# Decoder layer on one core: self-attention scores as one multiplication of 96 stacked rows per head with 256 columns each, and each unit one slot later

## The chip, the cores and the metric

One Trainium2 chip, one of its cores. The metric is the device time of one execution in microseconds (us); smaller is better.

## The reference

One pre-norm decoder layer in float32: x is (2, 1024, 512), the context (2, 2048, 512). The self-attention has 16 heads of 32 elements; each token sees only keys at an even distance of at most 16. Queries and keys are divided by their length before the scores.

```python
x = x + attn(layernorm(x))             # qkv projection, 16 heads, windowed softmax, output projection
x = x + cross_attn(layernorm(x), ctx)  # one head of 512, 1024 x 2048 scores per batch, full softmax
x = x + ffn(layernorm(x))              # silu(x wg) * (x wu), then wd; hidden size 1536

# inside attn, per head (d = 32):
q = q / (norm(q) + 1e-6); k = k / (norm(k) + 1e-6)
scores = q @ k.T                       # scale 1
allowed = (abs(j - i) <= 16) & ((j - i) % 2 == 0)
out = softmax(where(allowed, scores, -inf)) @ v
```

## The kernel before

The tokens are laid out so that even and odd positions are apart: four sequences (`NS` = 4 rounds, `s`) of 512 tokens (`SEQ`), in which the window is a plain band of 8 to either side. Each round has 16 heads in 4 groups of 4 (`g`), and 4 tiles of 128 keys (`i`). A **unit** is one group and one tile, `n = 4 g + i`; there are 16 units in a round and 64 in all. The key tile of a unit meets a window of 136 or 144 queries (`window(i)`).

Every float32 operand of a multiplication is split into a rounded part (`_h`) and its rest (`_l`), and a product is the sum of three: high by high, high by low, low by high (`three`, lines 189 to 191).

The program is written out by hand, engine by engine; each engine executes its own list in order, and waits on counted semaphores. The loop over the units is the skeleton: for each of TensorE (PE), VectorE (DVE), ScalarE (ACT), GpSimd (POOL) there is a **slot** `n` of round `s`, and each slot also holds pieces of other work:

- slots 0 to 3: `project_qk(s, 1, t)`, the second half of the round's query and key projection; 4 to 7: `project_v`, `project_out(s-1, t)` (the output projection of the round before), transposes of the next round's input; 8 to 11: `project_qk` of the next round, transposes for the cross-attention query; 12 to 15: `project_v` of the next round and `project_query(s-1, m)`; in the last round the first score blocks of the cross-attention (`cross.pe_scores`) start there.
- `heads(s, g)` turns a group's queries and keys on PE into two PSUM banks (`kt`, `qt`). `heads_hi` (ACT) and `heads_lo` (DVE) copy them out as high and low parts: `kt_h`, `kt_l`, and for the queries `qbd_h`, `qbd_l`, each in two copies that a mask (`hmask`) zeroes for every other head. Groups 2 and 3 are turned in slots 6 and 7, group 0 of the next round in slot 14, group 1 in slot 15.
- `scores(s, n)`: six multiplications. Two heads share 64 rows; the zeroed halves of `qbd` keep them apart. The pair for rows 0 to 63 and the one for rows 64 to 127 stand side by side, for each of the three products. Then `exp` (ACT) into `probs`, `mask` (POOL, line 508, times `band`), and `weighted(s, n)` (PE, lines 1179 and 1183): eight multiplications of 32 columns of the array, the values and the row sums.
- In slot `n` PE makes `scores(n + 1)` first and `weighted(n)` last; ACT and POOL likewise handle unit `n + 1`. Units 8 and the next round's 0 are made at the end of slots 7 and 15 (`LATE`).
- When a group is done, `copy_out` (ACT) takes sums and values to SBUF, `inverse` (DVE, line 906, two halves) inverts the sums, `out_scale` (POOL, line 517) multiplies, `out_hi` (ACT) and `out_lo` (POOL, line 522) split the result for `project_out`, which waits for the `out_lo` of group 3 of its round. `out_bias` (POOL, line 527) adds a bias to the residual rows; `root1` (POOL, lines 483 and 485) belongs to the next round's norm.
- `spread1`, `spread2` (DVE) are norm statistics, `scale_units` (POOL) divides by the lengths. The DMAs of the SP queue load `x_in` (next round's input), `xs` (residual rows), `ct_raw` (context) and store `x1_scratch`, `qp_scratch`. `cross.load_ct(sp, n)` waits for `ct_l` of block `n - 2`.

## Time and profile before

| what | value |
|---|---|
| runs | 1194.45 and 1193.20 us, median 1193.83 |
| profiled execution | 1193.53 us, span of its instructions 1191.5 us |
| self-attention with its projections | about 48 to 380 us of the span |
| PE busy | 97% of the span |
| granted TensorE clock | 0.991 of full speed on the mean |

The profiled execution is 2.0 us longer than its span. Busy time of PE counts multiplications whose ends are modelled and overlap; the distance between two starts tells more of its pace than the duration of one.

### The profile page before, as it was taken

To read this page: it belongs to the slowest core of one execution; us is meant where nothing else is said; L and a number is where in the kernel's file an instruction comes from. 1 tells how busy PE (TensorE), PEld (TensorE's weight loads), DVE (VectorE), ACT (ScalarE), POOL (GpSimd) and SP (SyncE) were. 2 spreads that over 40 slices of the span, in tenths; PEclk is the share of its full clock that TensorE was granted. 3 is DMA by queue.
4 is the path that set the end of the run, shared out by engine and by line. 5 is a ranking of instruction groups with operands and counts; after the bars stand their busy time and mean duration, and the time that the engine had idled before them with its cause. 6 is when DMAs were issued, how large, how long until landed. Compare 5 with 4: busy or idle time off the path is not lost.

```text
span 1191.5 us, 17227 instructions
## 1 busy us (share of the span) xinstructions
PE 1151.1 (97%) x6432; PEld 935.4 (79%) x6432; DVE 872.4 (73%) x1352; ACT 548.3 (46%) x862; POOL 431.7 (36%) x383
## 2 busy tenths in 40 slices
PE   7999999999989999999999997999999998999998
PEld 6777778777767888888888885878778887888886
DVE  6666675684684657876687798875899878888775
ACT  5354454455364345554445444554444445444431
POOL 1255765665753300200020034022445842444431
PEclk9899999999989999999999998999999999999999
DMA  8001010200133434333334332223311111511101
GB/s 292 9 28 45 10 63 1 80 37 23 50 111 130 166 132 142 115 101 142 121 125 149 116 121 73 80 80 123 124 54 54 54 53 63 170 53 53 53 18 71
DMA packets 53570, 103.88 MB, mean 87 GB/s; under 512 B 4848, under 2 KB 17136, under 8 KB 52464
## 3 DMA queue, kind: packets, MB, share of 16 engines
q1 hardware_dynamic: 53488, 102.78, 25.8%
q8 instruction: 52, 0.85, 0.3%
q14 instruction: 30, 0.25, 0.1%
HBM read 85.99 MB, written 16.78 MB: 86 GB/s over the span
## 4 chain that ended last, share of the span: by engine, by line
PE 81%; DVE 9%; ACT 4%; issue 3%; POOL 3%; ACTq 0%; DVEq 0%; POOLq 0%
PE work L189 15%; PE work L190 14%; PE work L191 14%; PE score L189 4%; PE score L190 4%; PE score L191 4%; PE score L2523 4%; PE score L2524 4%; PE score L2525 4%; PE score L1165 2%; PE work L2523 2%; PE work L2525 2%; PE work L2524 2%; PE score L1179 1%; PE work L1092 1%
## 5 line engine op out<-in xcount | busy, mean ns | idle before, releaser
L508 POOL TENSOR_TENSOR probs<-probs,band 128x544 f32<-128x544 f32 (+1 forms) x64 | 92.4, 1444 | 87.3 <-ACT probs L639 87.0
L2196 POOL TENSOR_TENSOR hid<-fg,hid 128x512 fp32r<-128x512 f32 x48 | 84.4, 1778 | 106.5 <-ACT hid L2263 106.5
L189 PE MATMUL score<-pt_h,cn_h 128*128 128x512 f32 x256 | 101.8, 398 | 9.5 <-DVE pt_l L1672 5.9
L1512 POOL TENSOR_TENSOR xr<-xr,bv_row 128x512 f32<-128x512 f32 x16 | 27.3, 1731 | 228.1 <-DMA xr<-x_scratch 228.1
L190 PE MATMUL score<-pt_l,cn_h 128*128 128x512 f32 x256 | 100.6, 393 | 0.0
L191 PE MATMUL score<-pt_h,cn_l 128*128 128x512 f32 x256 | 100.5, 393 | 0.0
L189 PE MATMUL work<-x_q_h,ct_h 128*128 128x512 f32 x256 | 100.3, 392 | 0.0
L191 PE MATMUL work<-x_q_h,ct_l 128*128 128x512 f32 x256 | 99.7, 389 | 0.0
L190 PE MATMUL work<-x_q_l,ct_h 128*128 128x512 f32 x256 | 99.7, 389 | 0.0
L2402 DVE SCALAR_TENSOR_TENSOR fx<-work,fx 128x512 f32<-128x512 f32 x96 | 65.7, 685 | 40.2 <-PE work L191 40.2
L189 PE MATMUL work<-wqkv_h,xt_h 128*128 128x512 f32 (+1 forms) x256 | 94.0, 367 | 0.0
L2523 PE MATMUL score<-fxt,w_hl 128*128 128x512 f32 x236 | 92.3, 391 | 1.5 <-DVE fxt L2350 0.8
L2525 PE MATMUL score<-fxt,w_hl 128*128 128x512 f32 x236 | 91.9, 389 | 0.0
L2524 PE MATMUL score<-fxt,w_hl 128*128 128x512 f32 x236 | 91.8, 389 | 0.0
L2184 POOL TENSOR_TENSOR wsum<-w_stage 128x256 f32<-128x256 f32 x24 | 18.4, 765 | 194.0 <-ACT w_stage L2220 138.3
L190 PE MATMUL work<-wqkv_l,xt_h 128*128 128x512 f32 (+1 forms) x256 | 87.5, 342 | 0.0
L191 PE MATMUL work<-wqkv_h,xt_l 128*128 128x512 f32 (+1 forms) x256 | 87.4, 342 | 0.0
L1566 ACT ACTIVATE x_pr<-x_s 128x512 f32<-128x512 f32 x52 | 33.0, 634 | 94.4 <-DVE x_s L1668 94.4
L2263 ACT CAST hid<-fg 128x512 fp32r<-128x512 f32 x48 | 29.7, 621 | 87.5 <-DVE fg L2387 52.8
L189 PE MATMUL work<-wd_h,hid 128*128 128x512 f32 x176 | 68.7, 391 | 0.6 <-DVE fx L2402 0.6
L1672 DVE TENSOR_TENSOR pt_l<-x_pr,pt_h 128x512 fp32r<-128x512 f32 x64 | 51.3, 802 | 24.4 <-ACT pt_h L1570 23.6
L191 PE MATMUL work<-wd_h,hid 128*128 128x512 f32 x176 | 68.5, 389 | 0.0
(254 smaller groups left out, 3176.1 us busy)
## 6 DMA issues: line engine op xcount, KB each, us to landing
ct_raw<-in_ctx_t SPq DMA_DIRECT2D x32, 512.0 KB, 4.6
cn_raw<-in_ctx_n SPq DMA_DIRECT2D x32, 512.0 KB, 3.8
w_stage<-in_wg_t SPq DMA_DIRECT2D x12, 512.0 KB, 4.1
w_stage<-in_wu_t SPq DMA_DIRECT2D x12, 512.0 KB, 3.8
wd_raw<-in_wd_t SPq DMA_DIRECT2D x12, 512.0 KB, 3.7
x_in<-in_x SPq DMA_DIRECT2D x16, 256.0 KB, 2.8
xs<-in_x SPq DMA_DIRECT2D x4, 1024.0 KB, 5.2
x_scratch<-xs SPq DMA_DIRECT2D x4, 1024.0 KB, 4.7
```

The costliest lines, as they stand in the source:

```text
L189: pe.matmul(out, hi_s, hi_m, start=first, stop=False)
L190: pe.matmul(out, hi_s, lo_m, start=False, stop=False)
L191: return pe.matmul(out, lo_s, hi_m, start=False, stop=last)
L508: PL.tensor_tensor(probs[:, n % 2, :, 0:w], probs[:, n % 2, :, 0:w], band[:, c0:c0 + w].unsqueeze(1).to_broadcast([P, HPG, w]), ALU.mult). ...
L1566: A.activation(pr[:, j % 2, :], s_at(j), ACT.Exp).then_inc(e_done, 1)
L1672: V.tensor_tensor(pt_l[:, j % 2, :], pr[:, j % 2, :], pt_h[:, j % 2, :].bitcast(F32), ALU.subtract)\
L2196: PL.tensor_tensor(hid[:, q, 1, :], g[:, q, :], hid[:, q, 0, :].bitcast(F32), ALU.subtract).then_inc(hidl_done, 1)
L2263: A.copy(hid[:, q, 0, :], g[:, q, :]).then_inc(hidh_done, 1)
L2402: V.scalar_tensor_tensor(xs[:, t, :], work[:, 2 + n % 2, :], WSCALE, xs[:, t, :], ALU.mult, ALU.add)\
L2523: PE.matmul(bank(key), w_h, x_h, start=first, stop=False, skip_group_check=True)
L2524: PE.matmul(bank(key), w_h, x_l, start=False, stop=False, skip_group_check=True)
L2525: last = PE.matmul(bank(key), w_l, x_h, start=False, stop=k == 1, skip_group_check=True)
```

## The change

The scores of one head become one multiplication. A new SBUF tensor `stack` holds, for each of the four heads, three blocks of 32 rows: on the key side high, low, high, on the query side high, high, low. One multiplication over these 96 rows gives the sum of the three products. It always has 256 query columns, and the exponential reads the window out of them. The blocks are put there by DMAs from the SP queue: `stack_heads(s, g, b)` issues 12 for each half `b` of the 512 columns (24 per group, 384 in all), each of 32 rows by 2 by 256 floats (64 KB). They wait until the group's `heads_lo` is done and until the scores of the group before have read that half. The masked copies and `hmask` are gone: ACT and DVE each handle one query tile where there were two.

Each unit's scores, exponential and mask stand one slot later, at the start of slot `n`; `weighted(n - 1)` is the last thing in slot `n`. `copy_out`, `inverse`, `out_scale`, `out_hi` and `out_lo` stand one slot later too. `out_bias`, `root1`, `project_out` and all other pieces stay in their slots.

```diff
@@ SyncE @@
+            def stack_heads(s, g, b):
+                k = group(s, g)
+                if b == 0:
+                    wait_freed(sp, ("qt", s, g))
+                if k:
+                    sp.wait_ge(s_ready, ST * (k - 1) + 3 + b)
+                c = slice(b * SEQ // 2, (b + 1) * SEQ // 2)
+                parts_of, (k_h, k_l, q_h, q_l) = turned_heads(g)
+                for h in range(HPG):
+                    r = slice(DH * h, DH * h + DH)
+                    for i, (of_k, of_q) in enumerate(((k_h, q_h), (k_l, q_h), (k_h, q_l))):
+                        sp.dma_start(stack[DH * i:DH * i + DH, h, :, c].bitcast(F32),
+                                     parts_of[r, of_k:of_q + 1:of_q - of_k, c].bitcast(F32)).then_inc(stacked[b], 16)
...
+                stack_heads(s, 3, 0)
+                if s == NS - 1:
+                    cross.load_ct(sp, 2)
+                stack_heads(s, 3, 1)
...
+                if s + 1 < NS:
+                    for b in range(2):
+                        stack_heads(s + 1, 0, b)
@@ GpSimd @@
                 for n in range(UN):
-                    if n not in LATE:
-                        mask(s, n + 1)
-                    if n == 1 and s:
+                    mask(s, n)
+                    if n == 2 and s:
                         out_scale(group(s, -1))
-                    if n == 2 and s:
+                    if n == 3 and s:
                         out_lo(group(s, -1))
                     if n in (2, 3) and s:
                         out_bias(s - 1, 2 * n - 4)
@@ ScalarE @@
-                A.copy(kt_h[:, g % 2, :], bank(("kt", s, g))).then_inc(kq_hi, 1)
+                A.copy(parts_of[:, k_h, :], bank(("kt", s, g))).then_inc(kq_hi, 1)
                 wait_filled(act, ("qt", s, g))
-                for j in range(2):
-                    A.mul(qbd_h[:, g % 2, j, :], bank(("qt", s, g)), hmask[:, j:j + 1]).then_inc(kq_hi, 1)
+                A.copy(parts_of[:, q_h, :], bank(("qt", s, g))).then_inc(kq_hi, 1)
...
-                        if n == 2 and s:
+                        if n == 3 and s:
                             out_hi(group(s, -1))
@@ VectorE @@
-                    if n in (0, 1) and s:
-                        inverse(group(s, -1), n)
+                    if n in (1, 2) and s:
+                        inverse(group(s, -1), n - 1)
@@ TensorE, scores @@
-                if i == 0:
-                    wait_freed(pe, ("qt", s, g))
+                if i < 2:
+                    pe.wait_ge(stacked[i], MOVED * (group(s, g) + 1))
...
-                for kt, qt, first_mm, last_mm in ((kt_h, qbd_h, True, False), (kt_h, qbd_l, False, False),
-                                                  (kt_l, qbd_h, False, True)):
-                    for a in range(2):
-                        r = slice(64 * a, 64 * a + 64)
-                        last = PE.matmul(out[a], kt[r, g % 2, c], qt[r, g % 2, :, lo:lo + w],
-                                         start=first_mm, stop=last_mm)
+                for h in range(HPG):
+                    out = scb[:, h // 2, SEQ // 2 * (h % 2):SEQ // 2 * (h % 2) + SEQ // 2]
+                    at = min(lo, SEQ // 2)
+                    last = PE.matmul(out, stack[0:3 * DH, h, 0, P * i:P * i + P], stack[0:3 * DH, h, 1, at:at + SEQ // 2],
+                                     start=True, stop=True)
@@ TensorE, slots @@
-                    if n not in LATE:
-                        scores(s, n + 1)
+                    scores(s, n)
...
-                    weighted(s, n)
+                    if n:
+                        weighted(s, n - 1)
+                    elif s:
+                        weighted(s - 1, UN - 1)
             s = NS - 1
+            weighted(s, UN - 1)
```

The program's order on PE, at the change from one slot to the next. Before:

```order
L1179 MATMUL score<-probs,v 32x144 x4
L1183 MATMUL score<-probs,ones 32x144 x4
L1165 MATMUL score<-qbd_h,kt_h 128x2x136 x2
L1165 MATMUL score<-qbd_l,kt_h 128x2x136 x2
L1165 MATMUL score<-qbd_h,kt_l 128x2x136 x2
L189 MATMUL work<-wqkv_h,xt_h 128x512
```

and in the changed kernel:

```order
L1206 MATMUL score<-probs,v 32x144 x4
L1210 MATMUL score<-probs,ones 32x144 x4
L1192 MATMUL score<-stack 128x256 x4
L189 MATMUL work<-wqkv_h,xt_h 128x512
```

Six multiplications in three pairs have become four single ones; the place between `weighted` and the projection is the same.

The order on POOL in slots 1 to 3 of a round after the first (`o_sc` is `out_scale`, `ot_l` is `out_lo`, `xs` is `out_bias`, `rstd` and `nb` are `root1`, `probs` is `mask`). Before:

```order
L517 TENSOR_TENSOR o_sc<-o_sc,rsum 128x512
L508 TENSOR_TENSOR probs<-probs,band 128x4x136
L522 TENSOR_TENSOR ot_l<-o_sc,ot_h 128x512
L527 TENSOR_TENSOR xs<-xs,ob_row 128x512 x2
L483 TENSOR_TENSOR rstd_155<-ve_153,mhalf 128x1
L485 TENSOR_SCALAR nb_157<-mv_151,rstd_155 128x1
```

and in the changed kernel:

```order
L554 TENSOR_TENSOR o_sc<-o_sc,rsum 128x512
L564 TENSOR_TENSOR xs<-xs,ob_row 128x512 x2
L520 TENSOR_TENSOR rstd_154<-ve_152,mhalf 128x1
L522 TENSOR_SCALAR nb_156<-mv_150,rstd_154 128x1
L545 TENSOR_TENSOR probs<-probs,band 128x4x136
L559 TENSOR_TENSOR ot_l<-o_sc,ot_h 128x512
```

`out_lo` of the last group, which followed `out_scale` and one mask, now follows two `out_bias` and one `root1` as well.

The order on the SP queue from the last part of round 0 to the first of round 1. Before:

```order
L429 DMA xs<-in_x 128x4x512
L392 DMA x_in<-in_x 128x512 x4
L396 DMA x_scratch<-xs 128x4x512
```

and in the changed kernel:

```order
L456 DMA xs<-in_x 128x4x512
L421 DMA stack<-heads_even 32x2x256 x12
L398 DMA x_in<-in_x 128x512
L421 DMA stack<-heads_even 32x2x256 x12
L421 DMA stack<-heads_ot 32x2x256 x24
L421 DMA stack<-heads_even 32x2x256 x24
L421 DMA stack<-heads_x2t 32x2x256 x24
L398 DMA x_in<-in_x 128x512 x3
```

The queue, which held nine issues there, now holds 24 more for every group.

## Rows read from the trace of the kernel before

**Rows 1.** The page: busy time of each engine, and the chain that ended last.
```profile
PE 1151.1 (97%) x6432; PEld 935.4 (79%) x6432; DVE 872.4 (73%) x1352; ACT 548.3 (46%) x862; POOL 431.7 (36%) x383
...
PE 81%; DVE 9%; ACT 4%; issue 3%; POOL 3%; ACTq 0%; DVEq 0%; POOLq 0%
```

**Rows 2.** Timeline of PE, end of slot 2, start of slot 3, round 2 (start, duration).
```profile
223.58 0.43 PE L1183 MATMUL score<-probs,ones 128*32 128x144 f32 x8
223.94 0.40 PE L1165 MATMUL score<-qbd_h,kt_h 64*128 64x272 f32 x2
...
224.52 0.50 PE L189 MATMUL work<-wqkv_h,xt_h 128*128 128x512 f32 x1
224.86 0.39 PE L190 MATMUL work<-wqkv_l,xt_h 128*128 128x512 f32 x1
```

**Rows 3.** Timeline of PE, where 256-column multiplications follow `weighted` directly.
```profile
204.92 0.39 PE L189 MATMUL work<-wqkv_h,xt_h 128*128 128x256 f32 x1
205.15 0.28 PE L190 MATMUL work<-wqkv_l,xt_h 128*128 128x256 f32 x1
205.26 0.28 PE L191 MATMUL work<-wqkv_h,xt_l 128*128 128x256 f32 x1
```

**Rows 4.** Timeline of PE: starts that later steps are measured against.
```profile
93.83 0.40 PE L1165 MATMUL score<-qbd_h,kt_h 64*128 64x288 f32 x2
...
125.94 0.40 PE L1165 MATMUL score<-qbd_h,kt_h 64*128 64x288 f32 x2
...
230.18 0.40 PE L189 MATMUL work<-wo_h,ot_h 128*128 128x512 f32 x1
230.42 0.40 PE L190 MATMUL work<-wo_l,ot_h 128*128 128x512 f32 x1
...
359.56 0.40 PE L1165 MATMUL score<-qbd_h,kt_h 64*128 64x288 f32 x2
```

**Rows 5.** Timeline of DVE, slots 1 and 2 of round 2.
```profile
220.89 1.74 DVE L906 RECIPROCAL rsum<-rsum 128x256 f32<-128x256 f32 x1
...
223.42 0.69 DVE L852 TENSOR_TENSOR qk<-work,qkb_row 128x512 f32<-128x512 f32 x1 [0.25 <-PE work L191]
224.04 0.69 DVE L815 BATCH_NORM_STATS2 stats<-x_in 128x6 f32<-128x512 f32 x1
```

**Rows 6.** Timeline of POOL, slots 1 to 3 of round 2.
```profile
222.71 1.29 POOL L517 TENSOR_TENSOR o_sc<-o_sc,rsum 128x512 f32<-128x512 f32 x1 [4.18 <-DVE rsum L906]
223.95 1.37 POOL L508 TENSOR_TENSOR probs<-probs,band 128x544 f32<-128x544 f32 x1
...
226.62 2.53 POOL L527 TENSOR_TENSOR xs<-xs,ob_row 128x512 f32<-128x512 f32 x2
229.11 0.55 POOL L483 TENSOR_TENSOR rstd<-ve,mhalf 128x1 f32<-128x1 f32 x1
229.75 0.27 POOL L485 TENSOR_SCALAR nb<-mv,rstd 128x1 f32<-128x1 f32 x1
```

**Rows 7.** Timeline of the SP queue: start, time to issue, count.
```profile
0.79 1.33 SPq L403 DMA_DIRECT2D x_in<-in_x  x3
...
230.90 0.33 SPq L392 DMA_DIRECT2D x_in<-in_x  x1
...
355.69 0.33 SPq L1445 DMA_DIRECT2D ct_raw<-in_ctx_t  x1
```

**Rows 8.** The page, DMA issues: count, KB each, median us to landing.
```profile
x_scratch<-xr SPq DMA_DIRECT2D x16, 256.0 KB, 2.1
```

**Rows 9.** Timeline of DVE, `heads_lo` of round 0 group 2 and round 1 group 0.
```profile
87.36 0.69 DVE L895 TENSOR_TENSOR kt_l<-work,kt_h 128x512 fp32r<-128x512 f32 x1 [0.98 <-ACT kt_h L628]
...
119.84 0.69 DVE L895 TENSOR_TENSOR kt_l<-work,kt_h 128x512 fp32r<-128x512 f32 x1
```

**Rows 10.** Windows: stretch, length, busy times, then PEclk, DMA share, GB/s.
```profile
345.00:349.00 4.00, 1.26 (x22) 0.84 (x22) 2.07 (x6) 3.35 (x6) 3.02 (x3) 1.00 0.00 0
...
351.00:355.00 4.00, 4.00 (x10) 3.17 (x11) 3.93 (x5) 1.81 (x4) 1.92 (x2) 0.50 0.00 0
```

More of the change, by code:

```diff
@@ L364, in attention_phase @@
     kq_hi = sem("kq_hi")
+    stacked = [sem(f"stacked{b}") for b in range(2)]
     s_ready = sem("s_ready")
@@ L554, in _ @@
                         root2(s - 1, n - 6)
-                    if n in (6, 9, 13):
-                        out_scale(group(s, n // 4 - 1))
-                    if n == 7:
-                        mask(s, 8)
                     if n in (7, 10, 14):
-                        out_lo(group(s, {7: 0, 10: 1, 14: 2}[n]))
-                    if n == 15 and more:
-                        mask(s + 1, 0)
+                        out_scale(group(s, {7: 0, 10: 1, 14: 2}[n]))
+                    if n in (8, 11, 15):
+                        out_lo(group(s, {8: 0, 11: 1, 15: 2}[n]))
             s = NS - 1
```

104 lines of the change are left out of this document (53 added, 51 removed).

## The prediction

> **What bounds the kernel now.** I read the page first: PE is busy 97% of the span and carries 81% of the chain that ended last [rows 1]. So a change on DVE, ACT, POOL or the DMAs counts only where PE comes to wait for it, and a change on PE counts in full. I then read PE's timeline by starts, because the durations overlap, and looked for the distance between neighbours. Last I read DVE, POOL and the SP queue in the slots where the change reorders them, against the moment at which PE needs the result.
>
> **PE itself.** From the row sums of `weighted` to the second multiplication of the next piece the profile has 223.58 to 224.86 = 1.28 us: 0.36 to the scores, 0.58 for them, 0.34 to the second projection multiplication [rows 2]. The three pairs of 64 rows are cheap, but they change the shape of the tile in use twice, and each change costs at both sides: the multiplications of 256 columns that follow `weighted` directly start 0.36 us after the row sums as well, are then 0.23 us apart once and 0.11 to 0.12 us after that [rows 3]. For the new form I take 96 rows to be the same kind of tile as 128 rows. Then the new form is 0.36 to the first of the four, 0.23 + 0.12 + 0.12 + 0.12 to the projection's start, and 0.24, the undisturbed distance of 512 columns [rows 4], to its second multiplication: 1.19 us, 0.09 less than now. Times 64 units that is 5.8 us. The eight units that stood at the end of slots 7 and 15 lose one more change of tile, 0.1 us on each of its sides by the same rows, 1.6 us. Together **-7 us**, all on the path. If 96 rows count as a shape of their own, the change into projection work stays (0.34 in place of 0.24, and 0.1 more ahead of it): 0.2 us x 64 = 13 us dearer than that, **+6 us**. I take -7: the only tiles in the rows whose change costs are those of 64 rows and of 32 columns, and 96 rows fit into neither half.
>
> The Trainium skill bears on this on both sides. Its page TensorEngine Tiling (Array Packing), section Key Properties, says that changing the tiling mode drains the engine; the 0.34 us above against 0.24 agrees. The Trainium skill's page TensorE: Matmul & The Clock Gate, Part 3, advises to put small contractions on separate row groups, where they run at once, which speaks against this change: by columns alone the old form streams 3 x 280 and the new one 4 x 256, 184 more, so by that rule alone the sum would have +5 us in place of -7.
>
> DVE and ACT lose one tile of 128x512 per group, 0.7 us each (one such piece takes 0.69 [rows 9]); they are not the bound, so I count that at nothing except in the latency of `heads_lo` below.
>
> **`out_lo` of the last group, in rounds 1 to 3.** `project_out` of slot 4 waits for it, and starts now at 230.18 with no wait [rows 4]. Now the halves of `inverse` lie in slots 0 and 1; the second starts at 220.89 and `out_scale` follows at 222.71 [rows 5, 6]. After the change the second half is in slot 2. There DVE takes up the projection's tile at 223.42, the statistics from 224.04 for 0.69 + 0.4 us, then the inverse for 1.74: it ends at 226.85 [rows 5]. POOL then makes `out_scale` (1.29), two `out_bias` (2.53), `root1` (0.87 from 229.11 to 229.98), `mask` of unit 3 (1.37), and only then `out_lo` (another 1.29) [rows 6]: 226.9 + 7.3 = 234.2. PE comes to `project_out` at 230.1 or a little before. That is a **wait of 4.0 us**. Round 1 has the same order and distances, 4.0; round 3 has neither statistics nor `root1`, and no value projection before `project_out`, 3.6. Sum **+11.6 us**. What is queued behind it on PE is the whole slot; the other engines run ahead only as far as their own waits let them, and PE has no work to give back, so none of it is recovered. Of this cost I am surest: it is order and durations.
>
> **The clock.** Between 345 and 349 us PE was busy for 1.26 of 4.00 us at full clock, and from 351 to 355 the granted clock was 0.50, 1.2 in place of 2.4 GHz, although PE was then fully busy: 10 multiplications in 4 us, where 0.24 us apart would be 16 to 17 [rows 10]. The fall cost some 2 us there. A wait of 4 us leaves PE idle more completely than that stretch, so I expect a fall after each of the three waits, **+2.8 us each, 8.4 us** (bounds 0 and 3.4).
>
> **The stacking DMAs.** The price of one issue: three in a row took 1.33 us, 0.44 each; one alone 0.33 [rows 7]. Landing: the smallest median beside 16 alike is 2.1 us, for 256 KB [rows 8]. The trace has no transfer from SBUF to SBUF and none of 32 rows. I take 0.42 per issue and 2.0 to land, so a half of a group is complete 12 x 0.42 + 2.0 = 7.0 us after SP may start (bounds, estimates from the same rows: 12 x 0.33 + 1.7 = 5.7, and a third above, 9.2), and the second half 5.0 us later.
> - Most groups have two slots between their release and their use, 8.2 us where a slot is 4.1 (12 multiplications at 0.24, 1.2 for `weighted`, scores and the changes between), or more. By 7.0 us they are in time, by 9.2 they are not.
> - Round 1 group 0: the key cast is followed by `heads_lo` at 119.84, the query part now ends about 121.2 [rows 9]. Half 0 lands at 128.2. PE gets there at about 125.2 (125.94 [rows 4], less the scores that stood in slot 15): 3.0 us, and the second half 1.0 more.
> - Round 0 group 2: 87.36 + 1.35 = 88.7 [rows 9], landed at 95.7, wanted at 93.83 [rows 4]: 1.9, and 0.9 for the second half, behind one load of `x_in`.
> - Round 0 group 3, second half: its slots are short in round 0 (unit 13 comes three slots after the first release, one of them without a 512-column projection, about 11 us; 5.0 + 5.0 + 2.0 are needed): 1.2, an estimate.
> - Round 3 group 3: the second half stands behind `load_ct(2)`, which waits for `ct_l` and was issued at 355.69 [rows 7]: 0.4 + 5.0 + 2.0 later is 363.1, and unit 13 is wanted at 359.56 [rows 4]: 3.5. The first half 0.7.
>
> Sum 12.3. The two longest may let the clock fall too (+3); older waits in those slots, as for the length scaling, are met by the new ones (-1, a guess). **+14 us**, bounds 5 and 30.
>
> What pages give for this: the Trainium skill, page SBUF — State Buffer, section Door 1, states that partitions 0 to 31 reach 8 of 16 ports, 189 GB/s at 1 MiB; by that the 768 KB of a half need an estimated 4.1 us, less than the issue. The same page of the Trainium skill, section The DMA setup-cost knee, gives 138 GB/s at 64 KB, by which a half moves for an estimated 5.7 us in place of 5.0 and the sum would be 3 us higher. No row here shows either rate.
>
> **The sum**, against the profiled execution's 1193.53 us (0.3 under the median, which is nothing here): -7 + 11.6 + 8.4 + 14 = +27, **1220 us**. Within about 2% of the median (1170 to 1217.7) a measurement of this kernel counts as no change; the forecast lies just beyond.
>
> **Rivals.**
> 1. *The transfers and the clock are milder.* Issues at 0.33 us or covered, and no falls: -7 + 11.6 + 5 = +10, 1203 us. For it: the SP queue issued one alone in 0.33 [rows 7]. Against: three in a row took 0.44 each, and a 4 us gap is long. Chance 0.25.
> 2. *The shorter scores win (the other side).* The place is the boundary of each slot on PE. If `out_lo` comes in time, because POOL's spans on the profile are rough and its wait is not what PE meets, and the halves land before use, only -7 remains: 1186.5 us. It decides if `out_lo` ends before 230.1, four us earlier than I work out. Against it stand 7.3 us of POOL pieces in a fixed order [rows 6]. Chance 0.1.
> 3. *SP becomes the bound of every group.* If a half takes over 8.2 us, all sixteen groups are late: 9.2 gives 1 to 2.5 us on each of some ten groups in addition to the listed ones, and several falls: 1193.5 + 27 + 20 = about 1240 us. For it: no row shows 32-row transfers, each reading and writing the same quarter of the partitions. Chance 0.13.
> 4. *The lost side-by-side pairs weigh more.* The new form has four multiplications in a row where three pairs stood; if the changes of tile stay as well (96 rows a shape of their own), the scores cost +6 in place of -7: 1233 us. Against: the rows show no other cost at full tiles [rows 3]. Chance 0.07. The rule on row groups in the Trainium skill's page TensorE: Matmul & The Clock Gate points the same way.
>
> **How the numbers follow.** The forecast (1210 to 1230) has 0.45. The range leaves out rival 2 and the far part of rival 3: 1198 to 1240. Faster by over 2% has no mechanism here, 0.02. Beyond 1217.7 lie about six tenths of the forecast, rivals 3 and 4 and nothing of 1: 0.27 + 0.13 + 0.07, rounded up to 0.50, because a fall of the clock at any further wait adds. Within 2%: 0.48.
>
> **What would show it.** In the changed profile: four score multiplications 0.12 us apart and 0.34 gone before the projection; `project_out` of slot 4 in rounds 1 to 3 waiting some 4 us for POOL's `ot_l`, with the granted clock at 0.50 after it; the SP queue with about 5 us per twelve issues; PE waiting on DMAs of `stack` at round 1's start, at round 0 group 2 and at round 3 group 3. After the self-attention all should be as before. I would be wrong if the `ot_l` wait is under 2 us (DVE or POOL not as late as worked out), or if waits on `stack` appear in every group.

## The result and the profile after

The changed kernel takes **1287.88 us** (median of 2 runs, 1287.73 to 1288.03) against 1193.83 before: a ratio of 1.0788, 95% interval [1.0762, 1.0814], 94 us more. That is outside the predicted 1198 to 1240.

The page of the changed kernel:

```profile
PE 1176.6 (91%) x6304; PEld 964.7 (75%) x6304; DVE 864.5 (67%) x1336; ACT 541.6 (42%) x846; POOL 430.5 (33%) x378
...
PE 66%; SPq 15%; DVE 9%; issue 4%; DMA 3%; ACT 2%; POOL 2%; ACTq 0%; DVEq 0%
...
L1192 PE MATMUL score<-stack 96*128 96x256 f32 x256 | 54.1, 340 | 79.3 <-DMA stack<-heads_even 39.9
...
stack<-heads_even SPq DMA_DIRECT2D x192, 64.0 KB, 2.1
```

PE fell from 97% to 91% of the span, and the chain that ended last, which ran 81% through PE, has a new link: SP's queue, 15% [rows 1]. The third line names who waits: the score multiplications, 79.3 us, for DMAs that fill `stack`. The landing of one such DMA takes 2.1 us, where I took 2.0 [rows 8].

The stretch from 28 us to the start of the last score unit, by windows (length; busy time of PE, PEld, DVE, ACT, POOL; then granted clock, DMA share, GB/s). Before:

```profile
28.00:366.80 338.80, 326.17 (x2700) 255.44 (x2698) 225.85 (x450) 164.48 (x290) 195.23 (x168) 0.98 0.13 43
```

and after:

```profile
28.00:468.20 440.20, 356.67 (x2592) 288.42 (x2591) 219.92 (x436) 159.24 (x276) 193.28 (x168) 0.88 0.35 90
```

All of the loss is in here: behind it 824.7 us are left before and 818.1 after. PE's idle time, length less busy, rose from 12.6 to 83.5 us: +71. The mean clock fell from 0.98 to 0.88. Taken stretch by stretch, PE was at 1.2 in place of 2.4 GHz for 13.7 us before and 102.4 us after, in 2 and in 18 stretches, of which 1.0 and 21.1 us coincide with its waits. Half of the rest is work not done: 6.3 and 40.6 us, so the clock cost +34. The third term is smaller. Take length less waits less that half as the **work** of the stretch: 319.8 us before, 316.3 after. This -3.5 is not the gain of the new scores alone: experiment 2, with the same program on PE and few waits, has 320.2, and why the changed kernel has 4 us less is not shown. (The stretch ends one slot later after the change, so it grew by 101 us where the whole kernel grew by 94.)

The queue that fills `stack`, SP's timeline of the changed kernel (start, time to issue, count), at the place shown in the order:

```profile
97.60 7.76 SPq L421 DMA_DIRECT2D stack<-heads_even  x12
105.45 0.53 SPq L398 DMA_DIRECT2D x_in<-in_x  x1
106.03 7.63 SPq L421 DMA_DIRECT2D stack<-heads_even  x12
...
249.13 16.32 SPq L421 DMA_DIRECT2D stack<-heads_even  x24
```

Twelve issues take 7.6 to 7.8 us where I had 5.0: 0.60 us each (median of all) and 0.04 between them, **0.64 from start to start** where [rows 7] gave 0.44 for three loads in a row. From its first issue to its last landing a half takes 9.0 to 10.8 us, 9.2 on the median, where I had 7.0. The 384 issues hold the queue for some 240 us.

What the scores see of it, PE's timeline in round 2:

```profile
266.94 1.01 PE L1192 MATMUL score<-stack 96*128 96x256 f32 x3 [4.27 <-DMA stack<-heads_even]
```

and the windows there:

```profile
262.00:266.00 4.00, 0.67 (x17) 0.39 (x16) 1.38 (x2) 1.59 (x3) 0.00 (x0) 1.00 0.44 99
266.00:270.00 4.00, 3.06 (x9) 2.67 (x10) 0.00 (x0) 0.65 (x1) 1.07 (x1) 0.51 0.71 279
```

The group's 24 DMAs were issued from 249.13 to 265.45; PE, 0.67 us busy in the four microseconds before, starts at 266.94 and finds the clock at 0.51.

The new scores by themselves, between waits (answers to [rows 2]):

```profile
171.84 0.43 PE L1210 MATMUL score<-probs,ones 128*32 128x144 f32 x8
172.20 0.74 PE L1192 MATMUL score<-stack 96*128 96x256 f32 x4
172.78 0.40 PE L189 MATMUL work<-wqkv_h,xt_h 128*128 128x512 f32 x1
173.01 0.40 PE L190 MATMUL work<-wqkv_l,xt_h 128*128 128x512 f32 x1
```

171.84 to 173.01 is 1.17 us: I had 1.19, against 1.28 before. `project_out` waited for `ot_l` only 2.7 us in all, where I had forecast 11.6.

### The profile page after: what moved, and what is told of

The parts are those of the page before. It is cut to its first block, busy times and chain, and to the rows that moved or that the text cites. A ratio compares the mean times of both kernels' runs of the same rounds, so it can differ in the third digit from the quotient of the medians.

```text
span 1286.3 us, 17359 instructions
## 1 busy us (share of the span) xinstructions
PE 1176.6 (91%) x6304; PEld 964.7 (75%) x6304; DVE 864.5 (67%) x1336; ACT 541.6 (42%) x846; POOL 430.5 (33%) x378
## 4 chain that ended last, share of the span: by engine, by line
PE 66%; SPq 15%; DVE 9%; issue 4%; DMA 3%; ACT 2%; POOL 2%; ACTq 0%; DVEq 0%
SPq L421 15%; PE work L189 12%; PE work L190 11%; PE work L191 11%; PE score L189 4%; PE score L190 4%; PE score L191 4%; PE score L2549 4%; PE score L2551 4%; PE score L2550 4%; PE score L1192 2%; PE work L2549 2%; PE work L2551 1%; PE work L2550 1%; DMA stack<-heads_even 1%
## 5 line engine op out<-in xcount | busy, mean ns | idle before, releaser
L1192 PE MATMUL score<-stack 96*128 96x256 f32 x256 | 54.1, 340 | 79.3 <-DMA stack<-heads_even 39.9
L1192 PEld LDWEIGHTS score<-stack 96*128 96x128 f32 x256 | 39.7, 217 | 95.9 <-DMA stack<-heads_even 39.3
L189 PE MATMUL work<-wqkv_h,xt_h 128*128 128x512 f32 (+1 forms) x256 | 97.2, 380 | 0.0
L190 PE MATMUL work<-wqkv_l,xt_h 128*128 128x512 f32 (+1 forms) x256 | 96.1, 375 | 0.0
L191 PE MATMUL work<-wqkv_h,xt_l 128*128 128x512 f32 (+1 forms) x256 | 95.1, 371 | 0.0
L883 DVE TENSOR_TENSOR qk<-work,qkb_row 128x512 f32<-128x512 f32 x32 | 22.0, 689 | 78.7 <-PE work L191 78.2
L675 ACT ACTIVATE probs<-score 128x544 f32<-128x544 f32 (+1 forms) x64 | 40.9, 638 | 79.1 <-PE score L1192 79.1
```

The lines of the kernel that those rows point to most:

```text
L189: pe.matmul(out, hi_s, hi_m, start=first, stop=False)
L190: pe.matmul(out, hi_s, lo_m, start=False, stop=False)
L191: return pe.matmul(out, lo_s, hi_m, start=False, stop=last)
L675: A.activation(probs[:, n % 2].rearrange("p (a h) w -> p a h w", a=2)[:, :, :, 0:w], scb.rearrange("p a (h w) -> p a h w", h=2)[:, :, :, o ...
L1192: last = PE.matmul(out, stack[0:3 * DH, h, 0, P * i:P * i + P], stack[0:3 * DH, h, 1, at:at + SEQ // 2], start=True, stop=True)
```

## The experiments

Theory A: SP's queue issues a stacking DMA every 0.64 us, a half is late by that, and the rest of the forecast holds. The first four runs take the change apart and measure the issue.

**1. The slots alone.** Of the change only this kind of edit, on all engines, with the old scores:

```diff
-                    if n not in LATE:
-                        scores(s, n + 1)
+                    scores(s, n)
```

> Only the second half of the change: units, `out_scale`, `out_lo`, `out_hi` and `inverse` one slot later, while the scores stay the six multiplications of before and nothing is stacked; it computes the whole layer. Theory A (the stacking transfers on SP made the loss, and the terms on record for the slots still hold): `project_out` of slot 4 waits for `out_lo` of the last group in rounds 1 to 3, 11.6 us of waiting and 8.4 us of clock, so about 1214 us, and no TensorE wait above 1 us on anything else that is new. Rival B (the slots cost nothing, because the last group's inverse and `out_lo` come in time): 1194 us. Rival C (the slots themselves make the loss, by a wait in every group): near 1288 us.

1207.26 us, ratio 1.0110 [1.0095, 1.0125]: **+13.5 us**. PE at `project_out` of slot 4 in round 2:

```profile
235.87 0.47 PE L189 MATMUL work<-wo_h,ot_h 128*128 128x512 f32 x1 [3.84 <-POOL ot_l L531]
```

and the windows from there:

```profile
236.00:240.00 4.00, 4.00 (x12) 3.09 (x13) 0.00 (x0) 0.00 (x0) 3.90 (x5) 0.63 0.02 8
240.00:244.00 4.00, 4.00 (x41) 3.26 (x40) 1.38 (x2) 3.06 (x6) 1.32 (x4) 0.94 0.01 4
```

The three waits are 3.83, 3.84 and 3.54 us, 11.2 in all, each with a fall of the clock behind it. B and C fall. But the falls are short: at 0.63 over four microseconds and 0.94 over the next four the engine loses 1.5 + 0.2 = 1.7 us. Waits of 0.7 and 2.9 us in round 3, which A had not listed, add to it.

**2. Scores and slots, the stack of the first group alone.**

```diff
                 k = group(s, g)
+                if k:
+                    return
```

> The changed kernel, but only the first group's 24 stacking DMAs are issued; the scores of the other 15 groups read that old data in `stack`, so the output is not the layer's. All else stands, the one multiplication of 96 rows by 256 columns per head and the late slots too. Theory A (the stacking DMAs, 0.64 us from start to start on SP's queue where I had taken 0.42, made the loss): the 79.3 us of TensorE waits at the scores and the 102 us at half clock go; what is left is the term for shorter scores, -7 us, and the term for `out_lo` and its clock, +20 us: about 1207 us, or 1187 us if `out_lo` comes in time here. Rival D (the 96-row multiplications cost more than the six they replace, by changes of tile shape that the profile does not show as busy time): above 1220 us with no waits at the scores. Rival C (the slots): near 1288 us.

1208.20 us, 1.0119 [1.0104, 1.0134], A's number. The order of GpSimd at the wait of round 2 (answers to [rows 6]):

```profile
232.12 1.29 POOL L556 TENSOR_TENSOR o_sc<-o_sc,rsum 128x512 f32<-128x512 f32 x1 [4.06 <-DVE rsum L938]
233.36 2.53 POOL L566 TENSOR_TENSOR xs<-xs,ob_row 128x512 f32<-128x512 f32 x2
235.85 0.55 POOL L522 TENSOR_TENSOR rstd<-ve,mhalf 128x1 f32<-128x1 f32 x1
236.50 0.27 POOL L524 TENSOR_SCALAR nb<-mv,rstd 128x1 f32<-128x1 f32 x1
236.73 1.34 POOL L547 TENSOR_TENSOR probs<-probs,band 128x544 f32<-128x544 f32 x1
238.02 1.26 POOL L561 TENSOR_TENSOR ot_l<-o_sc,ot_h 128x512 fp32r<-128x512 f32 x1
```

and PE there:

```profile
239.43 0.77 PE L189 MATMUL work<-wo_h,ot_h 128*128 128x512 f32 x1 [4.02 <-POOL ot_l L561]
```

This is the row of pieces worked out in the prediction, piece for piece, with the 4.0 us wait at its end; the three waits come to 11.6. Against experiment 1 the work of the stretch is 320.2 in place of 326.2 us: the new scores give back 6.0. (The figure is 320.2 to 321.7 in experiments 2, 3, 5, 6 and 10, which have the same scores, so it is good to some 1.5 us.) Their gain is eaten by the first group: its scores wait 6.4 us for 24 DMAs in a row, with a longer fall of the clock.

**3. `out_lo` first.**

```diff
-                    if n in (2, 3) and s:
+                    if n in (3, 4) and s:
```

> The kernel before this one (stack written for the first group alone, output not the layer's), with `out_bias` of the last round moved from slots 2 and 3 to slots 3 and 4, behind `out_lo` of the last group in GpSimd's order. If GpSimd's order of those operations is what makes `out_lo` late, as the prediction says, the waits of 4.0, 4.0 and 3.6 us at `project_out` of slot 4 shrink by the two or three `out_bias` ahead of it, and the time falls by 5 to 20 us below the kernel before this one; if `inverse` of the second half in slot 2 makes it late, or nothing waits there, the two are the same within 2 us.

1199.29 us, 1.0047 [1.0030, 1.0064], 8.9 below experiment 2. The `ot_l` waits fall from 11.6 to 5.2 us. GpSimd's order is the cause of that part; what is left I put down to the second `inverse` half in slot 2, which was not moved by itself.

**4. Forms of DMA.** Here `probe()` issues four of a form and waits for them:

```diff
                     sp.dma_start(xs[:], x_v[0]).then_inc(xs_landed, 16)
+                    probe()
```

> The kernel before, whole, with 44 more DMAs on SP's queue in a stretch of round 0 in which that queue is idle: four in a row of each of eleven forms, with a wait for all four behind each form, between free regions of SBUF and DRAM. It measures how long one issue occupies SP's queue and how far apart four of them start. Forms in order: 32 rows x 2 x 256 elements from rows 0-31 to 0-31 (the stacking form); the same to rows 0, 32, 64, 96; 32 x 256; 32 x 512; 32 x 4 x 512; 96 x 2 x 256; 128 x 2 x 256; 128 x 512; 128 x 4 x 256 to DRAM; 32 x 2 x 256 from DRAM; 32 x 4 x 512 from DRAM. Theory A1 (the issue's price goes with few rows, i.e. with how the transfer is spread): 32-row forms near 0.60 us, 96- and 128-row forms of the same or more bytes near 0.33 to 0.44 us. Rival A2 (it goes with the bytes or the pieces): 32 x 256 at half or a quarter of the stacking form, 128 x 2 x 256 four times it. Rival A3 (a floor of the queue for SBUF to SBUF, whatever the form): all eight SBUF to SBUF forms 0.60 us, those with DRAM at one end less.

SP's timeline, one line per form of four: 32 x 256, 32 x 512, 128 x 512 between places of SBUF, then the two from DRAM:

```profile
102.97 2.47 SPq L426 DMA_DIRECT2D x2t_h<-wk_l  x4
106.75 2.41 SPq L426 DMA_DIRECT2D x2t_h<-wk_l  x4
...
130.62 2.45 SPq L426 DMA_DIRECT2D x2t_h<-wk_l  x4
...
143.48 1.75 SPq L426 DMA_DIRECT2D x2t_h<-qp_scratch  x4
146.88 1.71 SPq L426 DMA_DIRECT2D x2t_h<-qp_scratch  x4
```

Eight times the bytes and four times the rows leave the median at 0.60 us for SBUF to SBUF; from DRAM it is 0.42. Three of the 32 issues between places of SBUF took 1.3 us. A1 and A2 fall; A3 stands so far. Neither smaller nor wider DMAs are cheaper to issue; only fewer of them would help.

The next four vary the count of issues and who waits for them.

**5. Half the issues.**

```diff
-                for h in range(HPG):
+                for h in range(HPG if k == 0 else 2):
```

> The changed kernel, but after the first group only heads 0 and 1 of a group are stacked: 12 DMAs for a group where the change has 24, 6 for a half; heads 2 and 3 are multiplied from the first group's data, so the output is not the layer's. Theory A (the loss is the time in which SP's queue issues, 0.64 us each): a half is complete after 6 x 0.64 + 2.05 = 5.9 us where it took 9.7, two halves after 9.7 where they took 17.4, and the scores want them about 10 and 15 us after SP may start: nearly all waits at the scores go, and the time is that of the kernel with the first group alone, 1208 us, up to 1215. Rival F (what costs is the hand-over itself, one wait for a landing per half, whatever the count): the waits stay at more than half of 79 us and the time is 1245 us or more.

1216.40 us, 1.0184 [1.0169, 1.0199]. The score waits are 14.3 us, 7.1 of which experiment 2 has too. The time is 1.4 us over A's upper end; F falls. Of the new waits, 5.2 us stand in round 3 before group 3, whose second half is issued behind the context tile. Fewer issues are also fewer bytes here; experiments 4 and 14 keep the two apart.

**6. All the issues, nobody waits.** Here `aside` is a region of DRAM.

```diff
-                        sp.dma_start(stack[DH * i:DH * i + DH, h, :, c].bitcast(F32),
+                        sp.dma_start(aside[k, b, h, i] if k else stack[DH * i:DH * i + DH, h, :, c].bitcast(F32),
```

> The changed kernel, but after the first group the 24 DMAs of each group go from the same sources into DRAM and the scores read the first group's data and wait for none of them (output not the layer's). SP's queue issues as many DMAs of as many bytes, at the same points; the only new waits are ScalarE's, for its sources to be read before it writes over them. Theory A (the loss is that the scores wait for `stack`): 1208 us as with the first group alone, SP again some 240 us in stacking issues. Rival G (the occupied queue delays the other transfers on it, `x_in`, `xs`, the context tiles, or the traffic slows other work): the waits for `xn` and for the context tiles grow and the time is above 1215 us.

1214.87 us, 1.0173 [1.0156, 1.0190]: 6.7 over experiment 2, so G has a part in it. It has one clear place in round 3, ACT's timeline:

```profile
367.72 1.04 ACT L1575 CAST x_q_h<-x_q_raw 128x1024 fp32r<-128x1024 f32 x1 [4.46 <-DMA x_q_raw<-qp_scratch]
368.67 0.62 ACT L679 ACTIVATE probs<-score 128x544 f32<-128x544 f32 x1
```

The load of `x_q_raw` stood behind 24 stacking issues and landed late, ACT waited in front of its exponential, and PE 5.24 us for that. About half of the 6.7 us lies there: experiment 2 has waits of 3.5 us at this place, and a shorter stretch at half clock. Most of the rest is `ot_l`, for which PE waits 4.3 and 4.7 us in rounds 2 and 3 in place of 4.0 and 3.5. Against 80 us for waiting scores, the occupied queue by itself costs 7.

**7. New scores in the old slots**, `stack` of the first group alone; in `scores`:

```diff
-                for kt, qt, first_mm, last_mm in ((kt_h, qbd_h, True, False), (kt_h, qbd_l, False, False),
-                                                  (kt_l, qbd_h, False, True)):
+                for h in range(HPG):
```

> The other half of the change by itself: the slots of the kernel before (scores one unit ahead, `out_*` and `inverse` where they stood), with the one multiplication of 96 rows by 256 columns for each head, fed from a `stack` written for the first group alone, so the output is not the layer's. My term of -7 us for shorter scores: 1187 us, plus what the first group's scores wait for their 24 DMAs (6.4 us of waits and about 3 us of clock in the run with the first group alone), so 1193 to 1197 us; by the records, the start of the last unit less the waits ahead of it and less half of the time at half clock is 7 us smaller than in the kernel before. Rival H (the 96-row form gains nothing, what it saves in columns goes in changes of tile shape): 1202 us, and the same difference is 0.

1200.20 us, 1.0048 [1.0034, 1.0063], 3 us above the upper end of what I expected. The stretch, and what follows the first group's wait (windows):

```profile
28.00:374.60 346.60, 325.98 (x2577) 264.66 (x2576) 215.79 (x436) 154.50 (x276) 194.29 (x168) 0.96 0.14 47
...
50.00:58.00 8.00, 1.29 (x7) 1.32 (x7) 0.00 (x0) 0.00 (x0) 0.00 (x0) 0.52 0.47 104
58.00:68.00 10.00, 8.89 (x42) 8.83 (x43) 1.42 (x4) 1.60 (x3) 0.73 (x1) 0.50 0.29 63
```

The first group waits 8.5 us here, until 56.7, and the clock stays at 0.5 until about 71; the kernel before is at half clock for 6.8 us at this place. Without waits and clock the stretch is 315.1 us against 319.8 before: the scores gain 4.7. By the time alone H (1202 us) would be nearer than my 1193 to 1197; it falls by this difference, which it put at 0. A gain of 5 us is lost at a single place.

**8. Through DRAM.** Each half is stored once and loaded from there:

```diff
-                for h in range(HPG):
-                    r = slice(DH * h, DH * h + DH)
-                    for i, (of_k, of_q) in enumerate(((k_h, q_h), (k_l, q_h), (k_h, q_l))):
+                of = heads_dram[k, b].rearrange("(h r) j c -> r h j c", r=DH)
+                for i, (of_k, of_q) in enumerate(((0, 2), (1, 2), (0, 3))):
+                    for j, of_j in enumerate((of_k, of_q)):
+                        sp.dma_start(stack[DH * i:DH * i + DH, :, j, c].bitcast(F32), of[:, :, of_j, :]).then_inc(stacked[b], 16)
```

> The changed kernel, whole output, but each group's split heads are stored to DRAM (one DMA of 128 rows for each half, two for group 3) and `stack` is filled from there with 6 DMAs of 32 rows x 4 heads x 256 for each half, 14 issues for a group in place of 24, 12 of them with DRAM as the source. Theory A (issue time): four DMAs in a row with DRAM as source started 0.46 us apart and those with SBUF as source 0.64, so a group takes 12 x 0.46 + 2 x 0.6 = 6.7 us of SP's queue in place of 15.4, and a half is complete 6 x 0.46 + 4.4 = 7.2 us after its buffer is free; the waits at the scores fall from 79 us to under 20, and the time is 1208 to 1225 us. Rival I (latency takes the place of issue time: heads of groups 0 and 2 are split only some 10 us ahead of their scores, and store, landing and load in series take 4 + 7 us): 1 to 4 us of waiting in eight groups with a fall of the clock behind each, 1230 to 1250 us.

1225.60 us, 1.0261 [1.0245, 1.0276], between the two theories, with 31.9 us of score waits in ten places, where A had under 20. Behind the first group's 5.0 us come 4.6 us at group 2 of round 0 and 5.5 at group 0 of round 1, where the heads are split only shortly before: latency, as I had it. It is 62 us faster than the change.

Three of the next four ask about the rest of the forecast and about a better version.

**9. More forms.** The frame is that of experiment 4.

```diff
+                         [(aside[j, one, 0:2, 0:256], src[one, 0:2, 0:256]) for j in range(4)],
+                         [(aside[j, 0:1, 0, :], src[0:1, 0, :]) for j in range(4)],
```

> The kernel before, whole, with 40 more DMAs on SP's queue in the stretch of round 0 in which it is idle, and 8 on ScalarE's. In the first such run every form with SBUF as its source started 0.62 to 0.68 us apart, whatever its rows and bytes, and every form with DRAM as its source 0.46. Theory K (the source decides): here all forms from SBUF, eight stacking DMAs in a row, 128 rows and 32 rows of 8 KB contiguous to DRAM, 32 x 2 x 256 to DRAM and one single row to DRAM, start 0.60 to 0.68 us apart; 32 x 2 x 256 from DRAM 0.46; a row that takes SBUF and DRAM as source by turns holds both values; from ScalarE's queue four stacking DMAs start 0.64 us apart too. Rival L (strided pieces decide, since all forms from SBUF so far were cut from a wider tile): the contiguous forms and the single row 0.33 to 0.46. A lone one in an idle queue, its queue's state aside: the kernel before issues lone stores from SBUF in 0.33 us, so 0.33 to 0.6.

SP's timeline: the stacking form; these two; 32 x 2 x 256 from DRAM; the first two of the row that takes SBUF and DRAM by turns:

```profile
101.29 2.51 SPq L427 DMA_DIRECT2D x2t_h<-wk_l  x4
...
125.24 1.75 SPq L427 DMA_DIRECT2D aside_scratch<-wk_l  x4
128.30 1.13 SPq L427 DMA_DIRECT2D aside_scratch<-wk_l  x4
130.35 1.73 SPq L427 DMA_DIRECT2D x2t_h<-aside_scratch  x4
133.66 0.56 SPq L427 DMA_DIRECT2D x2t_h<-wk_l  x1
134.26 0.58 SPq L427 DMA_DIRECT2D x2t_h<-aside_scratch  x1
```

With SBUF as the source the same 64 KB go to DRAM for 0.43 us, a single row for 0.25: K falls. L falls too, since the form at 0.43 is strided. A lone DMA from SBUF to SBUF took 0.64, a lone one from SBUF to DRAM 0.35. The row by turns did not hold both values: from DRAM 0.58 and 0.57 us, from SBUF 0.56 and 0.53. These were of 32 x 256, a form that was not issued from DRAM in a row by itself, so why they are not at 0.43 stays open. ScalarE's queue issued only DMAs to DRAM here, so its price for SBUF to SBUF had to wait for experiment 14.

**10. Two thirds of the issues.**

```diff
-                    for i, (of_k, of_q) in enumerate(((k_h, q_h), (k_l, q_h), (k_h, q_l))):
+                    for i, (of_k, of_q) in enumerate(((k_h, q_h), (k_l, q_h), (k_h, q_l))[:3 if k == 0 else 2]):
```

> The changed kernel, but after the first group only two of the three row blocks of `stack` are refilled, 16 DMAs for a group, 8 for a half; the third block, the high part of the keys with the low part of the queries, stays the first group's, so the output is not the layer's. A half is complete after 8 x 0.64 + 2.05 = 7.2 us, what the forecast took for it (7.0). It asks whether the other terms of the forecast hold once this one is as I took it: 1220 us, the first group's wait, waits of 1 to 4 us in some four groups, and 4.0, 4.0, 3.6 us at `project_out` of slot 4. Rival (the forecast was also wrong in how the halves line up with the scores): waits at the scores of over 25 us in all, over 1230 us.

1224.61 us, 1.0263 [1.0234, 1.0292]. PE's groups in the stretch (busy, mean ns, then idle before and its releasers):

```profile
L1192 PE MATMUL score<-stack 96*128 96x256 f32 x256 | 48.3, 312 | 25.2 <-DMA stack<-heads_even 14.5 <-DMA stack<-heads_ot 10.5
...
L189 PE MATMUL work<-wo_h,ot_h 128*128 128x512 f32 x48 | 21.6, 450 | 11.4 <-POOL ot_l L559 11.4
```

Once a half takes about what I took for it (6.5 us, median), the kernel comes out 4.6 us above the forecast, and `ot_l` waits 4.02, 3.82 and 3.54 us in the slots named there. Of the 25.2 us at the scores some 7 are the first group's, 18 the others', where the prediction had 12.3 for these. Round 1 group 0 and round 0 groups 2 and 3 are close (3.5, 3.5 and 2.4 us for 4.0, 2.8 and 1.2); round 3 group 3 has 8.2 for 4.2. The rival's waits of over 25 us are there, its 1230 us is not.

**11. The change with `out_lo` first**, the edit of experiment 3 on the whole change.

```diff
-                    if n in (2, 3) and s:
+                    if n in (3, 4) and s:
```

> The changed kernel with all its stacking, whole output, and `out_bias` of the last round moved from slots 2 and 3 to 3 and 4, behind `out_lo`. With the first group's data alone this gave 8.9 us (1208.2 to 1199.3). In the changed kernel TensorE waits only 2.7 us in all for `ot_l`, since it is late already from its waits for `stack`: if one wait hides the other, the time stays within 3 us of 1288; if the two add, it is 1279 us.

1287.26 us, 1.0789 [1.0759, 1.0820], the change's own time. PE's group at the scores, over the stretch:

```profile
L1192 PE MATMUL score<-stack 96*128 96x256 f32 x256 | 53.4, 336 | 80.0 <-DMA stack<-heads_even 40.4 <-DMA stack<-heads_ot 23.3 <-DMA stack<-heads_x2t 16.3
```

The waits for `ot_l` are gone and those at the scores stay. One had hidden the other.

**12. Through DRAM, `out_lo` first, context tile later.**

```diff
-                if s == NS - 1:
-                    cross.load_ct(sp, 2)
                 stack_heads(s, 3, 1)
                 if s == NS - 1:
-                    for n in range(3, 5):
+                    for n in range(2, 5):
```

> The way through DRAM (1225.6 us) with two more edits, whole output: `out_bias` behind `out_lo`, worth 8.9 us where the stacking did not bind, and in round 3 the context tile 2 issued behind both halves of group 3, where the second half stood behind it and TensorE waited 7.6 us for it. If both give what they gave or cost where they stood alone: 1208 us. If the waits left (4.6, 5.5, 3.4, 2.3 us in groups 0 and 2, store, landing and load in series) take their place: 1215 us or more. In neither case is it under the 1194 us of the kernel before.

1220.80 us, 1.0228 [1.0206, 1.0250]: 4.8 us of the 17 that I had hoped for. The wait in round 3 is 8.1 in place of 7.6 us. So the context tile's place in the queue was not its cause. I put it down to traffic, which no run varied by itself; the DMA view of 362 to 378 us (busy tenths of the 16 engines; issues, KB each, median us to landing):

```profile
DMA  2059999999999898999998999999899999999999
...
stack<-heads_scratch SPq DMA_DIRECT2D x12, 128.0 KB, 8.3
x_scratch<-xs SPq DMA_DIRECT2D x1, 1024.0 KB, 5.8
x_q_raw<-qp_scratch SPq DMA_DIRECT2D x1, 1024.0 KB, 7.7
ct_raw<-in_ctx_t SPq DMA_DIRECT2D x2, 512.0 KB, 8.6
```

All sixteen engines are full, and the twelve loads, issued behind 3 MB of others, take 8.3 us each to land against 3.6 over the whole run of experiment 8.

**13. What sets the price.** The frame of experiment 4 again.

```diff
+                forms = ([(aside[j, one, 0:2, c], src[one, 0:2, c]) for j in range(4)],
+                         [(flat[j], src[one, 0:2, c]) for j in range(4)],
```

> The kernel before, whole, with 42 more DMAs on SP's queue while it is idle in round 0, four of a form in a row: (1) 32 x 2 x 256 from SBUF to DRAM, pieces spaced as in SBUF; (2) the same to DRAM without spaces; (3) as 1 from rows 32 to 63; (4) as 1 with every second tile of the source; (5) 32 x 4 x 256 to DRAM; (6) 128 x 2 x 256 to DRAM; (7) 128 x 4 x 256 to DRAM; (8) one row of 512 from SBUF to SBUF; (9) the stacking form, SBUF to SBUF; (10) 32 x 2 x 256 from DRAM without spaces to SBUF; (11) two of 128 x 4 x 256 from DRAM to SBUF. Theory M (the price goes with whether the two ends have the same spacing or one queue's descriptors can be merged): 1 and 3 at 0.43, 2, 4 and 10 at 0.60, 8 at 0.25 and 9 at 0.60 although its ends are spaced alike, so M must fail at 9 unless SBUF to SBUF has a price of its own. Theory N (SBUF to SBUF has its own floor, and to DRAM the price goes with the pieces moved): 8 at 0.60, 9 at 0.60, 1 to 4 alike, 7 above 6 above 1. Theory O (the count of descriptors alone): 8 at 0.25, 1 to 4, 9 and 10 alike, 7 dearest.

SP's timeline: forms 2, 4, 5, 8, 9 and 10:

```profile
98.56 2.60 SPq L427 DMA_DIRECT2D aside_scratch<-wk_l  x4
...
106.30 1.74 SPq L427 DMA_DIRECT2D aside_scratch<-wk_l  x4
109.36 2.50 SPq L427 DMA_DIRECT2D aside_scratch<-wk_l  x4
...
127.74 2.70 SPq L427 DMA_DIRECT2D x2t_h<-wk_l  x4
131.60 2.66 SPq L427 DMA_DIRECT2D x2t_h<-wk_l  x4
135.72 2.47 SPq L427 DMA_DIRECT2D x2t_h<-aside_scratch  x4
```

Two prices recur, 0.43 and 0.60. Between places of SBUF even one row costs 0.60: N's floor stands, and O falls. With DRAM at an end it is 0.43 for two pieces a row spaced as in SBUF, 0.60 for four pieces a row (form 5) or for an end without spaces (2, 10). Form 5 speaks against M, forms 2 and 10 against N. Larger forms to DRAM took more: 128 x 2 x 256 up to 0.50 each, 128 x 4 x 256 0.59, 0.64, 1.05 and 1.39. No theory covers all eleven; the rule behind the prices stays open.

**14. Two queues.** The third row block goes to ScalarE's queue, with the edit of experiment 3:

```diff
+                for h in range(HPG):
+                    r = slice(DH * h, DH * h + DH)
+                    act.dma_start(stack[2 * DH:3 * DH, h, :, c].bitcast(F32),
+                                  parts_of[r, k_h:q_l + 1:q_l - k_h, c].bitcast(F32)).then_inc(stacked[b], 16)
```

> The changed kernel, whole output, with the third row block of `stack` (4 of the 12 DMAs of each half) issued on ScalarE's queue at the end of the slots in which SP starts the half, and `out_bias` of the last round behind `out_lo`. SP then issues 8 for a half as in the run with two thirds (1224.6 us), and the order of `out_bias` gave 8.9 us where stacking did not bind. If each queue pays its own issues and ScalarE has the time (46% busy before, 2.6 us more per half): 1216 us. Rival (ScalarE issues in order with its casts and exponentials, 2.6 us in each of two slots of four, and the scores' exponentials come late): waits of TensorE for `probs` and `v`, over 1235 us. Rival (both queues share one price): near 1287 us.

1218.70 us, 1.0219 [1.0199, 1.0239]: 2.7 us over my figure, with experiment 12 (1220.80) the fastest with the whole output and the new scores; their runs overlap. PE's group at the scores, and the issues on `stack` by queue (min/median/max ns):

```profile
L1205 PE MATMUL score<-stack 96*128 96x256 f32 x256 | 49.8, 319 | 24.0 <-DMA stack<-heads_even 11.4
L421 SPq DMA_DIRECT2D stack<-heads_even x128: 585/597/1993, 46.4 to 357.6; - x128
L674 ACTq DMA_DIRECT2D stack<-heads_even x64: 592/619/1755, 46.5 to 357.3; - x64
```

Each queue pays its own 0.60 to 0.62. Both rivals fall. All 384 DMAs with all their bytes are issued and waited for, as in experiment 11, and the waits at the scores fall from 80.0 to 24.0 us: it is the issue time in one queue that made them, and not the bytes. The kernel is still 25 us behind the kernel before.

## Why the prediction was wrong, point by point

**The step that failed** is "I take 0.42 per issue and 2.0 to land, so a half of a group is complete 12 x 0.42 + 2.0 = 7.0 us" (bounds 5.7 to 9.2). The landing was right. The issue is 0.64 from start to start, and a half is complete 9.2 us after its first issue (median; 11 x 0.64 + 2.05 = 9.1, since the landing is counted from the start of the last issue, and my sum added that issue's time once more). That is my upper bound, not beyond it; what was beyond the range is what such a half costs. The rows I took it from were loads from DRAM; the trace of before holds nothing from SBUF to SBUF, and I said so, but then took the nearest price for the price (experiments 4, 9, 13). The later sentence "Most groups have two slots [...] 8.2 us [...] by 9.2 they are not" held the truth. By time against count of issues for a half:

| issues for a half | half complete, us (median measured) | second half, us after (estimate, count x 0.64) | score waits, us | time, us |
|---|---|---|---|---|
| 0 | | | 7.1 | 1208.2 |
| 6 | 5.3 | 3.8 | 14.3 | 1216.4 |
| 8 | 6.5 | 5.1 | 25.2 | 1224.6 |
| 12 | 9.2 | 7.7 | 79.3 | 1287.9 |

From 0 to 8 an issue costs 2 us, from 8 to 12 it costs 16. The step lies between a half of 6.5 and one of 9.2 us. The queue may start when the third scores of the group before end, and the next are wanted at the start of theirs: at full clock 7.4 us (67.81 to 75.26 in the changed kernel), a little less than the two slots that I took.

**Rival 3** named this mechanism and priced it at 1240 us, from a half of 9.2 us and "1 to 2.5 us on each of some ten groups". What it missed is the second half. It stands behind the first in the same queue and is complete 7.7 + 9.1 = 16.8 us after SP starts, while the scores want it 7.4 + 4.1 = 11.5 after: an estimated 5.3 us late in each group. The changed kernel waits 2.4 to 6.9 us in each of groups 1 to 14, 4.5 on the mean, in its two halves together; 6.1 in the first group; and 9.6 in the last, where only 3.0 us lie between release and use and the second half stands behind the context tile: 79.3 in all. So 80 us is the right size, but 15 times 5.3 is near it partly by luck: most groups wait less (slots at half clock are longer), the first is not in it, and in every second group SP starts 2.5 to 5.2 us after the release, once `heads_lo` is done. The scores of a group and the queue wait for each other by turns over one buffer. A second `stack` buffer would cut that; it was not tried.

**The clock.** A fall does come behind each wait of 4 us, as I wrote, but it cost 1.7 us and not 2.8 (experiment 1). That the waits at the scores bring 16 more stretches at half clock was not in the sum beyond +3; it is +34 us.

**`out_lo`** was right in order, place and size: 11.2, 11.6, 11.6 and 11.4 us in experiments 1, 2, 5 and 10 against 11.6. In the changed kernel it is 2.7, since PE is late already (experiment 11). A cost worked out alone was no part of the sum any more once a larger one stood ahead of it. With its clock and the small waits in round 3 the slots cost 13.5 us where I had 20.

**The shorter scores** gained 6.0 us (experiment 2 against 1) and 4.7 (experiment 7) for -7. Ninety-six rows are no shape of their own, which was rival 4: the projection's second multiplication starts 0.23 us after its first behind them, and 0.34 behind the old form. The rule on small contractions in the Trainium skill, page TensorE: Matmul & The Clock Gate, Part 3, would keep them side by side on separate row groups; my estimate from it, by columns, was +5 in place of -7, and the trace does not agree.

**Not in the sum at all** was the first group. Nothing lies between its heads and its scores, and its 24 DMAs stand there whole: 4.8 to 8.5 us of waiting plus the clock behind it in every kernel that stacks from one queue. With two queues it was 0.7 (experiment 14).

**What the forecast would have been.** With the half about as I took it, experiment 10 measured 1224.6 for 1220; the other terms are 5 us off in all. That is a net figure and in part luck: the waits at the scores were 25.0 us for 12.3, the older waits that they replaced 6 for 1, and each fall of the clock was milder. The figure of the Trainium skill, page SBUF — State Buffer, section The DMA setup-cost knee, by which a half moves in an estimated 5.7 us, decided nothing: the twelve issues alone take 7.7 at 0.64 each, and experiment 4 shows the same price for eight times the bytes.

**Of the signs listed**, the score distance and the quiet remainder came true; the waits of 4 us for `ot_l` came only in kernels where the stacking did not bind (experiments 1, 2, 5 and 10); "if waits on `stack` appear in every group" was the one that proves me wrong, and it did.

## What to carry to other kernels

Before you replace compute with many small DMAs, count issues for each queue and period, take their price from transfers between the same two memories (or widen the range well past the nearest row when there are none), and follow the last one of the period, not the first: it carries the whole row. Near the point at which a batch takes as long as the slots it has, the cost is a step, not a slope, and the range of a forecast must reach across that step if a bound of the unknown does. A saving of 0.1 us in each of 64 units on the bound engine, 6 us measured, is worth about one wait of 4 us with the clock behind it, 5.7 us.

## What the hardware showed unasked

- A DMA from SBUF to SBUF is issued in 0.60 us on SP's queue (median, for 1 row or 128 and for 2 to 256 KB; experiments 4 and 13) and 0.62 on ScalarE's (64 KB, experiment 14); with DRAM at one end some forms take 0.43, but 0.57 where they took turns with the others (experiment 9).
- Behind a wait of 8.5 us on PE the clock stayed at 0.50 for another 14 us, with one wait of 1.1 us in them (experiment 7; the kernel before has 6.8 us at half clock there); behind waits of 3.8 us for less than four (experiment 1).
- A queue that only issues, with nobody waiting, still cost 7 us, about half of them through one load that stood behind it (experiment 6).
